# The end of a gated graph attention: X comes into TensorE's sum through a diagonal matrix, and ScalarE writes the sum to X

## The reference

```python
def _L0_xattn_ref(h, adj_raw, Wq, Wk, gamma_raw):   # h: ctx_512, adj_raw: layernorm(x)
    sim = jnp.einsum('bhnd,bhmd->bnm', Q, K) / (jnp.sqrt(jnp.float32(d)) * H)
    threshold = jax.lax.top_k(sim, 153)[0][:, :, -1:]
    A_learned = jax.nn.sigmoid(sim) * (sim >= threshold)
    A_learned = (A_learned + jnp.swapaxes(A_learned, -1, -2)) * 0.5
    gamma = jax.nn.sigmoid(gamma_raw)
    return (1.0 - gamma) * adj_raw + gamma * A_learned
...
x = x + jnp.tanh(g_xattn[0]) * _L0_xattn_ref(ctx_512, _layernorm(x), ...)
x = x + jnp.tanh(g_ffn[0]) * _L0_ffn_ref(_layernorm(x), ...)
```

## Time and profile before

| | us |
|---|---|
| median of 3 runs | 1746.77 |
| lowest and highest | 1746.47 and 1748.21 |
| the profiled execution, its own time | 1749.59 |
| its span in the profile | 1747.8 |
| TensorE busy in the span | 1670.6 |
| VectorE busy | 1504.4 |
| ScalarE busy | 1002.7 |

### The profile page before, as it was taken

One profiled execution on the slowest core, in us unless ns is written; L12 is line 12 of the kernel. 1 busy time (PEld: TensorE's weight loads), 2 busy tenths in 40 slices (PEclk: granted clock), 3 DMA queues, 4 the chain that ended last, 5 costly groups with the idle time before them and its releaser, 6 DMA issues.

```text
span 1747.8 us, 27857 instructions
## 1 busy us (share of the span) xinstructions
PE 1670.6 (96%) x9694; PEld 1172.0 (67%) x9744; DVE 1504.4 (86%) x2940; ACT 1002.7 (57%) x1816; POOL 808.1 (46%) x856
## 2 busy tenths in 40 slices
PE   8798899999978999999999999999999999999999
PEld 5577766666656666676665577787787778874443
DVE  6988889999998899999999877777777778878885
ACT  7888678858986222111111666566566666646664
POOL 3100022121221678666666776676676676666110
PEclk9999999999998999999999999999999999999999
DMA  9764116435762232323333522322323222233434
GB/s 326 263 205 164 37 62 162 107 73 118 169 157 97 65 110 75 91 67 86 80 79 106 157 85 76 95 65 81 97 65 81 82 66 76 53 106 88 93 88 106
DMA packets 157915, 186.05 MB, mean 106 GB/s; under 512 B 85584, under 2 KB 112464, under 8 KB 154576
## 3 DMA queue, kind: packets, MB, share of 16 engines
q1 hardware_dynamic: 146016, 153.00, 31.9%
q10 hardware_dynamic: 11760, 31.27, 6.1%
HBM read 110.83 MB, written 37.75 MB: 85 GB/s over the span
## 4 chain that ended last, share of the span: by engine, by line
PE 59%; DVE 7%; POOL 1%; issue 1%; ACT 1%; DMA 1%; SPq 0%; ACTq 0%; DVEq 0%
PE ps L2509 6%; PE ps L2498 5%; PE ps L2065 4%; PE ps L2567 4%; PE ps L2614 3%; PE ps L2616 3%; PE ps L2615 3%; PE ps L2569 3%; PE ps L2568 3%; PE ps L1629 3%; PE ps L1647 3%; PE ps L2020 3%; PE ps L1621 3%; PE ps L2022 2%; PE ps L2021 2%; PE ps L2043 2%
## 5 line engine op out<-in xcount | busy, mean ns | idle before, releaser
L2537 POOL TENSOR_SCALAR E<-E,ri 128x512 f32<-128x512 f32 x256 | 396.7, 1570 | 187.6 <-DVE ri L2532 187.6
L2307 POOL TENSOR_TENSOR R<-R,R 128x512 f32<-128x512 f32 x128 | 162.4, 1292 | 146.1 <-DVE R L2248 146.0
L2518 ACT ACTIVATE E<-ps,nm 128x512 f32<-128x512 f32 x256 | 175.3, 691 | 79.7 <-DVE nm L2525 79.7
L2632 ACT ACTIVATE TH<-ps 128x512 fp32r<-128x512 f32 x256 | 140.1, 601 | 135.0 <-PE ps L2509 135.0
L2683 DVE TENSOR_TENSOR TL<-ps,TH 128x512 fp32r<-128x512 f32 x256 | 165.2, 685 | 27.1 <-ACT TH L2632 25.7
L2127 ACT ACTIVATE KH<-ps 128x512 fp32r<-128x512 f32 x64 | 38.3, 598 | 243.3 <-PE ps L2045 233.7
L2525 DVE TENSOR_REDUCE nm<-ps 128x1 f32<-128x512 f32 x256 | 162.3, 678 | 8.7 <-PE ps L2498 8.7
L1563 POOL TENSOR_SCALAR sc<-sc,gs 128x1 f32<-128x1 f32 x32 | 15.0, 469 | 310.3 <-DVE sc L1432 310.3
L2509 PE MATMUL ps<-CST,E 128*128 128x128 f32 x1024 | 134.1, 273 | 3.2 <-POOL E L2537 1.7
L2509 PEld LDWEIGHTS ps<-CST,E 128*128 128x128 f32 x1024 | 118.9, 140 | 24.2 <-POOL E L2537 4.7
L1423 DVE SCALAR_TENSOR_TENSOR U<-fTH,sc,ps 128x512 f32<-128x512 f32 x128 | 94.9, 744 | 26.7 <-PE ps L1629 18.2
(11 more groups left out here) (274 smaller groups left out, 4522.8 us busy)
## 6 DMA issues: line engine op xcount, KB each, us to landing
wr<-in_wff SPq DMA_DIRECT2D x24, 1024.0 KB, 5.4
aw<-in_wff ACTq DMA_DIRECT2D x40, 512.0 KB, 4.5
scratch<-QS SPq DMA_DIRECT2D x128, 128.0 KB, 2.4
KS<-KP SPq DMA_DIRECT2D x64, 256.0 KB, 3.6
QR<-scratch SPq DMA_DIRECT2D x64, 256.0 KB, 3.5
keys<-KST SPq DMA_DIRECT2D x32, 256.0 KB, 3.3
KR<-keys SPq DMA_DIRECT2D x30, 256.0 KB, 3.8
wscr<-awb ACTq DMA_DIRECT2D x24, 256.0 KB, 3.0
```

Source lines behind the costliest of these rows:

```text
L2307: e.tensor_tensor(Q.r1[:, z, c, :], Q.r1[:, z, c, :], ask_r2(Q, n)[:, c, :], ALU.add).then_inc(S_["radd"].sem, 1)
L2518: e.activation(A.e[:, x % EB, :], K.PS[x % 4][:], ACT.Exp, bias=A.nm[:, c], accum_out=A.sm[:, c]).then_inc(S_["exp"].sem, 1)
L2537: e.tensor_scalar(A.e[:, x % EB, :], A.e[:, x % EB, :], A.ri[:, x % 8:x % 8 + 1], None, ALU.mult).then_inc(K.S["pl"].sem, 1)
```

## The change

TensorE now makes the whole sum of a tile but for xb. A diagonal matrix with xa on its diagonal times X opens the sum (new L429), a diagonal matrix with c times A follows (new L431), and the four transposed blocks are ordinary float32 products of A's blocks with that diagonal matrix (new L433), since a transpose can't scale. ScalarE reads the bank, adds xb and writes X (new L573); it is this now that frees the bank and tells x1. VectorE's 16 instructions L800 are gone, and so is the semaphore xg. GpSimd builds 17 diagonal matrices of 128 x 128, one for c and one for each tile in a ring of eight. The statistics for the tiles 0 to 3 move one step earlier in VectorE's list and wait for x1, and the fourth load of second-layer weights on SyncE waits for the sixteenth x1 where it waited for the sixteenth xg.

```diff
     def symmetric(*tiles):
...
-            w.wait_ge(S_["a2"], 4 * b + 4)
-            w.wait_ge(S_["d_cst"], 16)
             w.wait_ge(S_["sime"], 16)
             w.wait_ge(S_["x1"], t - 3 if t < 8 else t - 1 if t > 9 else 0)
+            w.wait_ge(S_["diag"], t + 2)
+            w.wait_ge(S_[f"d_x{b}"], 16)
+            e.matmul(bank[:], F.diag[:, t % 8, :], K.X[:, t, :], start=True, stop=False)
+            w.wait_ge(S_["a2"], 4 * b + 4)
+            e.matmul(bank[:], F.diag[:, 8, :], F.a2[b % 2][:, i, :], start=False, stop=False)
             for j in range(4):
-                e.matmul(bank[:, 128 * j:128 * j + 128], F.a2[b % 2][:, j, 128 * i:128 * i + 128], K.ident, is_transpose=True, start=j == 0, stop=False)
-            e.matmul(bank[:], K.ident, F.a2[b % 2][:, i, :], start=False, stop=True).then_inc(S_["sym"].sem, 1)
+                m = e.matmul(bank[:, 128 * j:128 * j + 128], F.a2[b % 2][:, j, 128 * i:128 * i + 128], F.diag[:, 8, :], start=False, stop=j == 3)
+            m.then_inc(S_["sym"].sem, 1)
...
     def back(*tiles):
         for t in tiles:
             w.wait_ge(S_["cb"], 1)
-            w.wait_ge(S_[f"d_x{t // 4}"], 16)
-            w.wait_ge(S_["xs"], t + 1)
-            e.activation(K.X[:, t, :], K.X[:, t, :], ACT.Identity, bias=F.xb[:, t:t + 1], scale=F.xa[:, t:t + 1]).then_inc(S_["xg"].sem, 1)
+            w.wait_ge(S_["sym"], t + 1)
+            e.activation(K.X[:, t, :], sym_bank(PS, t)[:], ACT.Identity, bias=F.xb[:, t:t + 1]).then_inc(S_["x1"].sem, 1)
...
-    def back(*tiles):
-        for t in tiles:
-            w.wait_ge(S_["xg"], t + 1)
-            w.wait_ge(S_["sym"], t + 1)
-            e.scalar_tensor_tensor(K.X[:, t, :], sym_bank(PS, t)[:], K.cc[:, 1:2], K.X[:, t, :], ALU.mult, ALU.add).then_inc(S_["x1"].sem, 1)
...
         elif late == 2:
-            back(0, 1, 2, 3)
+            feed0_stats(e, w, dc, K, F0)
         elif late == 3:
-            feed0_stats(e, w, dc, K, F0)
+            feed0_factors(e, w, dc, K, F0)
...
+    e.tensor_scalar(F.diag[:, 8, :], K.ident, K.cc[:, 1:2], None, ALU.mult).then_inc(S_["diag"].sem, 1)
+    for t in range(NT):
+        w.wait_ge(S_["sym"], t - 7)
+        e.tensor_scalar(F.diag[:, t % 8, :], K.ident, F.xa[:, t:t + 1], None, ALU.mult).then_inc(S_["diag"].sem, 1)
...
-        w.wait_ge(S_["xg"], 16 if i == 3 else 0)
+        w.wait_ge(S_["x1"], 16 if i == 3 else 0)
```

More of the change, by code:

```diff
@@ L252, in __init__ @@
         self.sd = M.tile([128, NT], F32, "sd")
+        self.diag = M.tile([128, 9, 128], F32, "DIAG")
         at = M.top
@@ L622, in front_scalar @@
         elif late == 1:
-            back(0, 1, 2, 3)
+            back(0, 1)
+        elif late == 2:
+            back(2, 3)
         elif late == 3:
-            sigmoid(8, 9, 10, 11)
+            sigmoid(8, 9)
+            back(4, 5)
+            sigmoid(10, 11)
     sigmoid(12)
-    back(4)
+    feed0_high(e, w, K, F0, 0)
+    back(6)
     sigmoid(13)
[L629 to L633, removed]
+    back(7)
+    sigmoid(14, 15)
     feed0_high(e, w, K, F0, 1)
@@ L636, in front_scalar @@
     feed0_whole(e, w, K, F0, 0)
-    back(7, 8)
     feed0_codes(e, w, K, F0, 0)
@@ L640, in front_scalar @@
     feed0_silu(e, w, K, F0, 0)
-    back(9)
     feed0_silu(e, w, K, F0, 1)
-    back(10)
-    feed0_abs(e, w, K, F0, 0)
-    back(11, 12, 13, 14)
+    back(8, 9)
     feed0_scaled(e, w, K, F0, 1)
@@ L649, in front_scalar @@
     feed0_silu(e, w, K, F0, 3)
-    back(15)
+    back(10, 11)
+    feed0_abs(e, w, K, F0, 0)
     feed0_high(e, w, K, F0, 2)
+    back(12, 13, 14, 15)
     feed0_abs(e, w, K, F0, 1)
@@ L866, in front_vector @@
             held = None
-    feed0_factors(e, w, dc, K, F0)
     feed0_norm(e, w, K, F0, 0)
@@ L871, in front_vector @@
     feed0_scale(e, w, dc, K, F0, 0)
-    back(4)
     feed0_low(e, w, K, F0, 1)
-    back(5, 6, 7)
     kept(8, 9, 10)
@@ L880, in front_vector @@
     feed0_norm(e, w, K, F0, 2)
-    back(8)
     kept(12, 13, 14)
-    back(9)
     rows0(4)
@@ L886, in front_vector @@
     rows0(5)
-    back(10, 11)
     feed0_low(e, w, K, F0, 2)
-    back(12)
     rows0(6)
     feed0_norm(e, w, K, F0, 3)
-    back(13)
     gate_up(e, w, K, F0, 2)
-    back(14)
     rows0(7)
-    back(15)
     rows0(8)
@@ L936, in front_gpsimd @@
     e.tensor_scalar(F.xa[:], F.xa[:], 1.0, None, ALU.add).then_inc(S_["cb"].sem, 1)
+    w.wait_ge(S_["cb"], 1)
+    w.wait_ge(S_["d_cst"], 16)
+    e.tensor_scalar(F.diag[:, 8, :], K.ident, K.cc[:, 1:2], None, ALU.mult).then_inc(S_["diag"].sem, 1)
+    for t in range(NT):
+        w.wait_ge(S_["sym"], t - 7)
+        e.tensor_scalar(F.diag[:, t % 8, :], K.ident, F.xa[:, t:t + 1], None, ALU.mult).then_inc(S_["diag"].sem, 1)
 def front_done(w, K):
     w.wait_ge(K.S["sym"], NT)
-    w.wait_ge(K.S["xg"], NT)
     w.wait_ge(K.S["x1"], NT)
@@ L1436, in feed0_stats @@
     for i in range(4):
+        w.wait_ge(K.S["x1"], i + 1)
         row_stats(e, w, dc, F.nm, K.X, i, K.S["ns0"])
```

## The result

The changed kernel takes 1767.3 us (median of 4 runs, 1765.87 to 1768.42); the kernel before took 1746.71 beside it (4 runs, 1746.47 to 1748.21). The ratio is 1.0111 [1.0099, 1.0123]: 20.6 us slower, against a forecast of 1767.4 and +20.6. That the two agree to a tenth is luck: terms of the sum were off by up to 1.6 us, and they cancelled.

A forecast was written before the change was run, and what follows sets the result against it. TensorE before 254 was taken to set when the long VectorE-bound stretch begins, and added TensorE time to be paid beyond small waits. 8.1 - 0.6 + 10.5 + 2.4 + 0.2 = +20.6 on 1746.77 gives 1767.4 us; range 1760 to 1772.

The forecast's parts named there:

- TensorE's additions: TensorE, each of sixteen symmetric tiles: a tile goes from 1.30 to 2.61 us, +1.31; sixteen make +21.0.
- The Trainium skill's rule: Rival for the symmetric tiles: plain products cost four times the transposes, 14 us more, 1781; chance 2%.
- The first eight tiles: TensorE up to the first norm's transposes: 10.5 us more, less waits of 0.30, 0.35 and 1.76, makes +8.1.
- The clock between 212 and 222: TensorE at the first feed-forward tile: the fall to the low clock comes later or not at all, -0.6 (0 to -1.3).
- The other eight tiles: TensorE's full stretch from 222 on: 8 x 1.31 us is paid in full, +10.5.
- the turn of the codes of tile 1: Gate 4, after the last symmetric product: TensorE waits for ScalarE's copy, now queued behind tile 15's write; +2.4 us.
- VectorE: Before 262: the sixteen removed instructions, 11.9 us, are worth nothing, since VectorE waits for TensorE.
- GpSimd: Seventeen diagonal builds, some 0.6 us each, nine beside VectorE's bisection: +0.2, within 0 to 5.
- ScalarE falls behind: Rival, last six tiles: each waits 0.75 us for ScalarE to free its bank, +4.5, 1772; chance 6%.
- SyncE: Fourth weight load: starts some 25 us later, its first reader has over 10 us in hand; costs nothing.
- Made good later: Rival, 262 to 500: up to 6.8 us of lateness comes back through TensorE's slack, 1760.6; chance 9%.

The follow-up runs named there:

- e2: Changed kernel, but the diagonals hold xa / c, ScalarE multiplies by c as it empties the bank, and TensorE transposes again; 1760.19 us, ratio 1.0084.
- e3: Kernel before, plus one TensorE product of a zero matrix and A in each symmetric tile's sum; 1755.60 us, ratio 1.0055.
- e10: Changed kernel with nine small float32 products of ones on TensorE after the last symmetric product, filling the 2.39 us pause; 1767.0 us, ratio 1.0116.
- e4: Kernel before, with VectorE's 16 sums L800 made for only 8 of the 512 columns; 1747.94 us, ratio 1.0007.
- e6: Changed kernel with seventeen more builds of a diagonal on GpSimd, ahead of the real ones; 1767.04 us, ratio 1.0107.
- e1: Changed kernel with ScalarE's copy of the turned codes of tile 1 moved ahead of the write of tile 15; 1766.94 us, ratio 1.0118.
- e9: Changed kernel with the edits of e5 and e2 together; 1756.40 us, ratio 1.0054.
- e5: Changed kernel with ScalarE's copy of the turned codes ahead of tile 15's write and the two feed0_abs spread apart; 1767.73 us, ratio 1.0112.
- e8: Kernel before with small float32 products of ones in TensorE's three pauses around the first feed-forward tiles; 1745.56 us, ratio 0.9986.
- e7: Kernel before, but for tiles 8 to 15 ScalarE scales the sigmoid by c, GpSimd adds A, TensorE only transposes; 1752.42 us, ratio 1.0022.
- e11: Kernel before, unchanged, run once more for a second profile; 1750.35 us.

## Why the prediction was right, and where it was not

**TensorE's additions.** +1.31 a tile was right: a tile takes 2.60 (194.44 to 197.04) where it took 1.30. e2 and e3 measure the halves as 7.2 and 10.2. e3's is below 16 x 0.86 = 13.8, since the waits of 0.30, 0.35 and 1.76 take up the first 2.4 of it, and 1.1 comes from the clock, which didn't fall there: 10.3. The Trainium skill's rule that the float32 transpose mode is four times as fast ("TensorE: Matmul & The Clock Gate", Terms) is not what runs here: 0.90 against 0.44 is twice, and e2 says the same for sixteen tiles.

**The first eight tiles.** +8.1 predicted. The norm's transposes stand 28.46 behind LATE's `total` (218.39 - 189.93) against 20.20 of the earlier trace rows: +8.3. The `total`s are 7.1 apart rather than 7.0.

**The clock between 212 and 222.** -0.6 predicted within 0 and -1.3. From the norm's transposes to the turn of the first codes it was 7.96 us and is 6.87: -1.1. The profile of the changed kernel had no fall from 212 to 230; e10, the same program up to that place, had one from 225 on. The term was a chance, and belongs to the scatter.

**The other eight tiles, and the pause.** From the turn of the codes to the first V<-U it was 35.6 and is 50.4: +14.8. Of these 10.5 are the tiles, as predicted. The pause is 2.55 (257.74, where tile 15's last product is through, to 260.29), predicted 2.4, and the clock behind it takes some 1.6 more (10.5 + 2.55 + 1.6 = 14.65, and 0.15 stays open), which the prediction did not have. The step "the turn of the codes of tile 1" named the wrong instruction. It said that gate 4 waits, and that the norm's transposes still fill 0.44 of the time. In fact these transposes wait themselves: they write PS[0], where the turned codes lie until ScalarE has copied them. They sat ahead of gate 4 in a queue that is served in order, so the effect is nearly the same: gate 4 (260.97) stands 71.04 behind LATE's `total` where it stood 50.77, +20.3 against +20.4 predicted. The 2.4 was right for a reason that was only half right.

**VectorE.** 11.9 us for nothing: e4 shows it for 8.3 of them. **GpSimd.** 0 rather than +0.2, by e6. **ScalarE falls behind.** It does not: its longest idle times are waits for the symmetric products (3.76 and 2.20 us), not the other way round. **SyncE.** No wait for the weights appears.

**Made good later.** The rival at 9% said up to 6.8 in 262 to 500 by slack in TensorE. Nothing comes back there: the distance is +22.0 at the first V<-U and +22.1 at the last addition of that part. But 1.2 us come back right behind it, from 557 on, and not by slack: before, the clock fell after the pause there (fifteen products in 4.31 us), and in the changed kernel it did not (3.40). From the last addition to the last of these groups of products it is 12.1 to 12.3 us in the changed kernel, e1, e2, e3, e6, e9 and e10, and 13.2 to 13.6 in the two profiles of before, e4, e5 and e8 (e7 has 12.5). Another 0.4 comes back somewhere behind.

So the sum is 8.3 - 1.1 + 14.8 = 22.0, of which 1.5 comes back: 20.5. The prediction had 20.6 without the clock's 1.6 behind the new pause, without the 1.2 that the clock gave back at 557, and with half a microsecond too little for the clock at 212. These terms cancelled. The sum is also that of one pair of profiles; e11 shows that another profile of before moves it by 2 us at the first V<-U and by 3.7 at the end. What stands on firmer ground is the size of TensorE's term, which e2 and e3 measure, and the ratio of the runs.

## What to carry to other kernels

In this kernel TensorE had some tenths of a us free in each step, and work moved onto it was paid in full after those tenths, while work taken from VectorE beside it was worth nothing. So find the last wait before the next bound stretch, and count only that engine. A new pause on TensorE costs its length and possibly a stretch at the lower clock behind it; look for all pauses of a stage together, since e10 filled one and had its fall at another, while e8 filled three and had none up to 300. And before a us or two in one profile is explained, look at a second profile of the same kernel: anchor both at an event that the change cannot have moved.

## What was not expected of the hardware

**The scatter between runs goes with the clock.** For the 17 runs of the kernel before beside e1 to e4, the mean granted clock of a run and its time have a correlation of -0.92: 1742.5 to 1745.7 us at 0.992 and 0.993, 1747.0 to 1751.2 at 0.987 to 0.989, about 1.1 us for each 0.001. In 22 more beside e5 to e8 it is -0.87. The program decides where the pauses are; which of them is followed by a stretch at 1.2 GHz differed from one execution of the same instructions to the next.

This gives two estimates, both from runs that need not be of one chip. The five runs of before with 0.992 beside e1 to e4 took 1744.5 to 1745.7, and the four of the changed kernel, all with 0.992, have their median at 1767.3: at an equal clock the change costs about 22 us, as at the first V<-U, and the 20.6 of the medians holds a lower clock of before. And e5's runs, with 0.989 and 0.990, would be some 2.7 us faster at 0.992 by the 1.1 us for each 0.001, which is about the 2.5 that its order saves at the first V<-U.

**What a fall costs.** Where it came, one window of 5 us often stood at 0.66 (changed kernel and e6 260 to 265; e1, e5 and e10 225 to 230; e2 220 to 225; e11 210 to 215); elsewhere it lay across two, as at 0.75 and 0.90 in e9 from 220 to 230. The same product took 1.72 instead of 1.03, and the chain lost about 1.6 us in the changed kernel, 1.2 to 1.3 at 557. e3 has the pauses of the kernel before around the first feed-forward tiles and showed no window below 1.00 between 215 and 265.
